# The second MLP of a two-block transformer kernel: both layers as float32r products with sign weights, the second layer turned round

## What is computed

```
def _binarize(w):
    alpha = mean(abs(w), axis=1, keepdims=True)
    bw = alpha * sign(w)
    return w + stop_gradient(bw - w)

def _L1_ffn_ref(x, w1, b1, w2, b2):          # w1 (1024, 256), w2 (256, 1024)
    h = einsum('bsd,hd->bsh', x, _binarize(w1)) + b1
    h = gelu(h, approximate=False)
    return einsum('bsh,dh->bsd', h, _binarize(w2)) + b2

h = _layernorm(x) * (1 + cb) + sb
x = x + gb * _L1_ffn_ref(h, ...)
```

## Time and profile before

| | |
|---|---|
| median of 3 runs | 4103.46 us |
| the profiled execution's own time | 4113.75 us |
| its span, first to last instruction | 4112.0 us |
| mean granted PE clock | 0.918 |
| `mlp1` (b, 0), first product to last | about 34 us, 8 times |
| `mlp1` (b, 1), first product to last | about 38 us, 7 times, with `light` between |
| `mlp1` (7, 1), alone | about 30 us |

### The profile page before, as it was taken

The page is one execution under the profiler, slowest core; times in us unless marked ns, Lnnn a source line. Parts: engine busy times, 40 slices in busy tenths (PEclk is TensorE's granted clock), DMA queues, the critical chain, the costliest instruction groups (busy, mean ns, idle before and its releaser), DMA issues. The chain is left out here.

```text
span 4112.0 us, 81800 instructions
## 1 busy us (share of the span) xinstructions
PE 3470.7 (84%) x30905; PEld 2015.9 (49%) x30905; DVE 2448.6 (60%) x6156; ACT 1925.4 (47%) x4523; POOL 1483.3 (36%) x1807
## 2 busy tenths in 40 slices
PE   7368789997799888997899878998799988999787
PEld 3235544554446544465445544465444654456444
DVE  6755758367563767457573665637674565737652
ACT  5124435554264444554364542654445443645433
POOL 4223442244323442234423543334522444235311
PEclk9579899998899989998999988999999988999889
DMA  7210240002300221002300023002300024000220
GB/s 241 75 37 14 56 109 23 14 28 48 109 17 24 55 79 52 16 12 63 109 16 25 16 64 94 18 22 55 105 26 15 12 63 110 15 25 22 60 65 6
DMA packets 233602, 207.38 MB, mean 50 GB/s; under 512 B 13776, under 2 KB 214224, under 8 KB 233176
## 3 DMA queue, kind: packets, MB, share of 16 engines
q1 hardware_dynamic: 229168, 192.61, 16.9%
q0 software_dynamic: 3328, 8.39, 0.8%
q10 hardware_dynamic: 720, 1.15, 0.1%
HBM read 123.83 MB, written 77.69 MB: 49 GB/s over the span
## 5 line engine op out<-in xcount | busy, mean ns | idle before, releaser
L2379 ACT ACTIVATE arena<-pb 128x512 f32<-128x512 f32 (+3 forms) x1536 | 664.6, 492 | 240.3 <-PE pb L1605 232.7
L2459 POOL TENSOR_TENSOR arena<-arena,small 128x512 f32<-128x512 f32 x256 | 287.0, 1124 | 461.0 <-DVE small L1781 459.6
L2208 ACT ACTIVATE arena<-arena,small 128x256 f32<-128x256 f32 x512 | 255.8, 500 | 387.4 <-DVE small L1764 387.0
L1605 PE MATMUL pb<-arena 98*32 98x512 bf16 (+3 forms) x4608 | 397.7, 339 | 28.4 <-ACT arena L2379 21.7
L1563 PE MATMUL pb<-arena 96*32 96x128 bf16 (+5 forms) x5280 | 369.3, 278 | 58.5 <-DVE arena L2063 24.0
L1623 PE MATMUL pb<-arena,v 128*17 128x512 f32 (+3 forms) x3072 | 381.7, 497 | 26.8 <-POOL arena L2623 17.4
L2623 POOL TENSOR_SCALAR_AFFINE_SELECT arena<-arena 128x256 f32<-128x256 f32 x512 | 217.2, 428 | 462.6 <-ACT arena L2379 459.4
L2063 DVE TENSOR_REDUCE arena<-pb 128x1 f32<-128x512 f32 x512 | 333.3, 684 | 83.3 <-PE pb L1563 81.9
L1764 DVE CUSTOM_DVE_ANT_0 arena<-pb,wmask 128x256 f32<-128x256 f32 x512 | 195.8, 419 | 223.8 <-PE pb L1300 212.4
L1563 PEld LDWEIGHTS pb<-arena 96*32 96x32 bf16 (+1 forms) x5280 | 184.1, 101 | 254.4 <-issue 79.1
L1300 PE MATMUL pb<-arena 128*128 128x256 f32 x1024 | 276.6, 394 | 4.8 <-issue 3.6
(11 more groups left out here) (332 smaller groups left out, 7006.9 us busy)
## 6 DMA issues: line engine op xcount, KB each, us to landing
arena<-split_q SPq DMA_DIRECT2D x64, 384.0 KB, 3.8
arena<-split_k SPq DMA_DIRECT2D x24, 768.0 KB, 6.6
split_q<-arena SPq DMA_DIRECT2D x64, 192.0 KB, 2.3
split_q<-arena SPq DMA_DIRECT2D x96, 128.0 KB, 2.0
split_k<-arena SPq DMA_DIRECT2D x64, 192.0 KB, 2.4
split_k<-arena SPq DMA_DIRECT2D x96, 128.0 KB, 2.1
arena<-split_k SPq DMA_DIRECT2D x24, 384.0 KB, 8.1
xn<-h_d SPq DMA_DIRECT2D x8, 1024.0 KB, 8.8
```

The lines of the kernel that those rows point to most:

```text
L1605: mm = t.matmul(bank[bk][r:r + 32, 0:w_], ka[slot(c, g)][0:KA, h, kt_ * P + r:kt_ * P + r + 32], qa[slot(c, g)][0:KA, h, q0:NH], start=Tru ...
L2208: ins = s.activation(pm[n % 3][:, j], sm[n % 2][:, j], ACT.Exp, bias=nmx[:, 2 * sl + j:2 * sl + j + 1], scale=-1.0, accum_out=sml[:, 2 * s ...
L2379: s.activation(pp[pn % 4][:, h % 2, 0:w_], bank[n % 3][:, 0:w_], ACT.Exp).then_inc(a_exp1, 1)
L2459: g.tensor_tensor(pm[n % 3], pm[n % 3], rcl[:, 2 * sl:2 * sl + 2].unsqueeze(2).broadcast_to([P, 2, 2 * P]), ALU.mult).then_inc(p_norm0, 1)
```

## The change

- `two_valued` no longer forms sign times alpha: it copies the bf16 signs over w; POOL's ten additions, the `wtmp` buffers and one wait in each turn go. The turned weights are written as float32r, alpha is kept in a tile of its own.
- The modulated input is written as float32 (`hT2x`), copied by ACT to float32r (`hT2h`), and DVE writes the remainder as float32r (`hT2l`).
- First layer: for each block four products of 128x512 in float32r (two pieces, high part and remainder) in place of two in float32. ACT's Gelu has alpha as its scale and writes `gt` (two buffers). The result is copied to float32r `gh` (by ACT for c = 0, by DVE for c = 1), and DVE writes the remainder `gl`; both have three buffers.
- Second layer: two blocks behind the first. The sign weights are stationary and `gh`, `gl` move: four products of 128x512 for each block, summed over the eight blocks in two banks (0 and 1 for c = 0; 5 and 6 for c = 1). ACT copies the two sums with alpha into `moT`, PE turns them back in two groups of four, DVE multiplies by the gate and POOL adds, each 128x512, twice instead of four times 128x256.
- The first layer has two banks for c = 0 as before, and one bank (7) instead of three for c = 1.
- The list of steps is the same.

```diff
@@ two_valued (DVE)
-                        v.wait_ge(b_alpha, 2 * m + 2)
-                        if m >= 2:
-                            v.wait_ge(b_add, m - 1)
-                        else:
-                            v.wait_ge(r_h[0], 16 * 2)
-                        v.scalar_tensor_tensor(out=wtmp[m % 2][:, 0:width], in0=sgn[:, c0:c0 + width], scalar=ac, in1=w, op0=ALU.mult,
-                                               op1=ALU.subtract).then_inc(b_sign, 1)
+                        v.tensor_copy(w, sgn[:, c0:c0 + width]).then_inc(b_add, 1)
@@ POOL
-                for m, (w, width, _) in enumerate(BINARY):
-                    g.wait_ge(b_sign, m + 1)
-                    g.tensor_tensor(w, w, wtmp[m % 2][:, 0:width], ALU.add).then_inc(b_add, 1)
@@ banks
-        MLP1_BANKS = {0: (6, 7), 1: (7, 5, 6)}
+        MLP1_NORM, MLP1_W1, MLP1_SUM, MLP1_TURN = ({0: (6, 7), 1: (7, 5)}, {0: (6, 7), 1: (7,)}, {0: (0, 1), 1: (5, 6)}, {0: (6, 7), 1: (7, 5)})
@@ mlp1 (PE)
+                    for m in range(FT + 2):
+                        if m < FT:
+                            bk = MLP1_W1[c][m % len(MLP1_W1[c])]
+                            for w in left[bk]:
+                                t.wait_ge(*w)
+                            for k in range(KD):
+                                t.matmul(bank[bk], w1s[:, k, m * P:(m + 1) * P], hT2h[:, k], start=k == 0, stop=False)
+                                mm = t.matmul(bank[bk], w1s[:, k, m * P:(m + 1) * P], hT2l[:, k], start=False, stop=k == KD - 1)
+                            mm.then_inc(t_w1, 1)
+                            left[bk] = [(a_g, FT * H + m + 1)]
...
+                        if m >= 2:
+                            k = m - 2
+                            t.wait_ge(gl_set, FT * H + k + 1)
+                            for d in range(KD):
+                                t.matmul(bank[sums[d]], w2s[:, k, d * P:(d + 1) * P], gh[:, k % 3], start=k == 0, stop=False)
+                                mm = t.matmul(bank[sums[d]], w2s[:, k, d * P:(d + 1) * P], gl[:, k % 3], start=False, stop=k == FT - 1)
+                            mm.then_inc(t_w2, 1)
+                        yield
...
+                    for u in range(2):
+                        bk = MLP1_TURN[c][u]
                         for w in left[bk]:
                             t.wait_ge(*w)
...
+                        t.wait_ge(a_mo, KD * H + KD)
+                        for i in range(2):
+                            for d in range(KD):
+                                mm = t.transpose(bank[bk][:, (KD * i + d) * P:(KD * i + d + 1) * P], moT[:, d, (2 * u + i) * P:(2 * u + i + 1) * P], ident[:, :])
+                        mm.then_inc(t_mo, 1)
@@ norm_half (DVE); ACT writes hT2x[:, 0] and hT2h
+                    v.tensor_scalar(hT2x[:, 1], bank[banks[1 % len(banks)]], modc[:, 5 * KD + 1, b:b + 1], modc[:, 4 * KD + 1, b:b + 1],
+                                    ALU.mult, ALU.add).then_inc(v_nx, 1)
+                    for k in range(KD):
+                        v.wait_ge(a_n2, KD * H + k + 1)
+                        v.tensor_tensor(hT2l[:, k], hT2x[:, k], hT2h[:, k].bitcast(F32), ALU.subtract).then_inc(v_n2, 1)
@@ mlp1 (DVE)
+                    for m in range(FT + 2):
+                        k = m - 1
+                        if c == 1 and 0 <= k < FT:
+                            v.wait_ge(a_g, FT * H + k + 1)
+                            if k >= 3:
+                                v.wait_ge(t_w2, FT * H + k - 2)
+                            v.tensor_copy(gh[:, k % 3], gt[:, k % 2]).then_inc(gh_set, 1)
+                        if 0 <= k < FT:
+                            v.wait_ge(gh_set, FT * H + k + 1)
+                            if k >= 3:
+                                v.wait_ge(t_w2, FT * H + k - 2)
+                            v.tensor_tensor(gl[:, k % 3], gt[:, k % 2], gh[:, k % 3].bitcast(F32), ALU.subtract).then_inc(gl_set, 1)
+                        yield
@@ mlp1 (ACT)
+                    for m in range(FT + 2):
+                        if m < FT:
+                            s.wait_ge(t_w1, FT * H + m + 1)
+                            if m >= 2:
+                                s.wait_ge(gl_set, FT * H + m - 1)
+                            gelu_tables[0] = True
+                            s.activation(gt[:, m % 2], bank[MLP1_W1[c][m % len(MLP1_W1[c])]], ACT.Gelu, scale=alpha[:, m:m + 1],
+                                         bias=cols[:, C_FB1 + m:C_FB1 + m + 1]).then_inc(a_g, 1)
+                        if c == 0 and m < FT:
+                            s.wait_ge(a_g, FT * H + m + 1)
...
+                            s.activation(gh[:, m % 3], gt[:, m % 2], ACT.Copy).then_inc(gh_set, 1)
+                        yield
```

More of the change, by code:

```diff
@@ L10 @@
 BF16 = mybir.dt.bfloat16
+F32R = mybir.dt.float32r
 I32 = mybir.dt.int32
@@ L1462, in norm_half @@
                         mm.then_inc(t_n2, 1)
[L1463 removed]
+                        left[bk] = [(v_nx if k else a_nx, H + 1)]
                         yield
@@ L1691, in mlp1 @@
                     H = 2 * b + c
[L1692 to L1697, removed]
+                    yield from norm_half(b, c, MLP1_NORM[c])
+                    t.wait_ge(v_n2, KD * H + KD)
+                    sums = MLP1_SUM[c]
+                    for m in range(FT + 2):
[8 more added lines that the diff above has]
+                            left[bk] = [(a_g, FT * H + m + 1)]
+                        if m == 2:
+                            for bk in sums:
+                                for w in left[bk]:
+                                    t.wait_ge(*w)
+                                left[bk] = None
+                        if m >= 2:
[6 more added lines that the diff above has]
+                        yield
@@ L1698, in mlp1 @@
+                    for d in range(KD):
+                        left[sums[d]] = [(a_mo, KD * H + d + 1)]
+                    yield
+                    for u in range(2):
+                        bk = MLP1_TURN[c][u]
                         for w in left[bk]:
                             t.wait_ge(*w)
-                        for k in range(KD):
-                            mm = t.matmul(bank[bk], w1T[:, k, m * P:(m + 1) * P], hT2[:, k], start=k == 0, stop=k == KD - 1)
-                        mm.then_inc(t_w1, 1)
@@ L1720, in mlp1 @@
+                        for i in range(2):
+                            for d in range(KD):
+                                mm = t.transpose(bank[bk][:, (KD * i + d) * P:(KD * i + d + 1) * P], moT[:, d, (2 * u + i) * P:(2 * u + i + 1) * P], ident[:, :])
+                        mm.then_inc(t_mo, 1)
+                        left[bk] = [(v_w2, 2 * H + u + 1)]
+                        yield
+                    for _ in range(3):
                         yield
@@ L2299, in norm_half @@
                         yield
-                    s.wait_ge(t_n2, 2 * H + 1)
-                    s.activation(hT2[:, 0], bank[banks[0]], ACT.Identity, scale=modc[:, 5 * KD, b:b + 1], bias=modc[:, 4 * KD, b:b + 1]).then_inc(a_n2, 1)
+                    s.wait_ge(t_n2, KD * H + 1)
+                    if c == 0:
+                        s.wait_ge(split_out[1][1], 16 * SPLIT_DMAS * (b + 1))
+                    s.activation(hT2x[:, 0], bank[banks[0]], ACT.Identity, scale=modc[:, 5 * KD, b:b + 1], bias=modc[:, 4 * KD, b:b + 1]).then_inc(a_nx, 1)
                     yield
+                    for k in range(KD):
+                        s.wait_ge(v_nx if k else a_nx, H + 1)
+                        s.activation(hT2h[:, k], hT2x[:, k], ACT.Copy).then_inc(a_n2, 1)
                     yield
@@ L2640, in mlp1 @@
                     add_bias(b, c, rows[:, R_B2:R_B2 + D], gates[:, 3])
[L2641 removed]
+                    for _ in range(FT + 2):
                         yield
[L2643 removed]
+                    for _ in range(3):
                         yield
[L2645 to L2647 removed]
+                    for u in range(2):
+                        x = xt[:, TH * c + 2 * u:TH * c + 2 * u + 2]
+                        g.wait_ge(v_w2, 2 * H + u + 1)
+                        g.tensor_tensor(x, x, xadd2[u], ALU.add).then_inc(p_w2, 1)
                         yield
+                    yield
                 take({"start": start, "light": light, "hrows": hrows, "heavy": heavy, "chain": chain, "att": att, "mlp1": mlp1,
```

114 lines of the change are left out of this document (52 added, 62 removed).

## The result

The changed kernel takes 4154.89 us (median of 4 runs, 4149.61 to 4161.64) where the kernel before takes 4105.26 (4 runs on the same chip, 4096.63 to 4116.93): ratio 1.0109, 95% interval 1.009 to 1.0128. It is slower by 1.1%, outside the predicted range of 4048 to 4126. The profiled execution took 4161.64 us, with a span of 4159.9 (before: 4112.0).

What follows compares the result with a forecast made beforehand. PE was taken to bind beside attention, with ACT next to binding beside light. Setup -3.5, attention -48, light +41 and last half -1 made -11.5 from 4103.5, 4092, lowered to 4089 us for hand-over; range 4048 to 4126.

Steps and rivals of the forecast that it cites:

- Which stretches bind, and the sign of each: Halves beside attention: PE binds, its saving counts, -48 us; beside light ACT is next to binding, new waits cost, +41.
- One pass for float32r: PE's first- and second-layer products: a 512-column float32r product takes one pass, 0.216 us, against 0.86 for float32.
- Setup, -3.5: Setup: POOL's 1024-wide additions, which hold up DVE, both go, saving 3.5 us.
- Beside attention, 5.9 to 7.4 earlier at POOL's last addition, 52 in eight halves: Eight halves c = 0: eleventh fill and POOL's last addition come 5.9 to 7.4 us earlier in the layout.
- I take off 0.5 for a lower clock after it: After each half c = 0, PE is less busy and the clock lower: 0.5 us off the gain, leaving 6 us x 8.
- The lead at POOL's last addition taken as the lead of all that follows: After each half c = 0: the lead at POOL's last addition, less 0.5 for clock, counts fully in the total, -48 us.
- Beside light, layout +31: Seven halves c = 1: one-bank and hand-over waits make the ninth scores 0.7 to 5.9 us later each, +31 in all.
- Its clock ... may fall in part of them; I add 1.5 a half: Halves beside light: PE idles three times for 3 to 4 us; clock and DVE meeting POOL add 1.5 each, +10.
- Last half, -1: Half (7, 1), running alone with one bank: second layer nearly hidden, -1 us in all.
- Hand-over, -3: PSUM hand-over, perhaps counted 0.1 us too high at eight places in 15 halves (-6 or so): forecast lowered from 4092 to 4089.
- rival 3: Beside light the clock falls (granted under 0.9), 36 us in seven halves instead of 10: total 4115 to 4129; chance 0.12.
- 14 for clock and contention together: Allowances: 0.5 us per half after attention for clock; 1.5 per half beside light for clock and DVE meeting POOL, +10.

Runs made afterwards that it cites:

- zgap: Changed kernel plus ten unread zero-weight products on PE before each c = 1 first-layer block that would wait behind an exponential round: 4126.16 us, 1.0036 of before.
- zgap_late: Changed kernel plus the zero-weight products of zgap and two unread products beside each first fill of attention halves c = 1 from the eighth: 4105.3 us, 0.9985 of before.
- c0_late: Kernel before with the new form in halves c = 0 alone, plus two unread products beside each first fill of c = 1 from the eighth: 4068.77 us, 0.9899.

## Why the prediction was wrong

- **Which stretches bind, and the sign of each.** Right: beside attention PE's saving counts, beside light it doesn't and the new waits cost.
- **One pass for float32r.** Right: 0.23 us a product, 0.216 assumed.
- **Setup, -3.5.** Right in kind: the operation that was L911, now L909, takes at most 0.285 us in its 19 rounds (2.21 before), and the first turn is 1.9 us earlier.
- **Beside attention, 5.9 to 7.4 earlier at POOL's last addition, 52 in eight halves.** Right: 53.1, and the half takes 30.1 to 31.5 us (29 to 31 stated).
- **"I take off 0.5 for a lower clock after it".** This step failed: the clock took 16.1 us in seven halves, 2.3 each, in the stretch from the row copy to the sixth maximum. I had looked at the stretch after the half for what DVE does, and taken its 0.92 as a state that stays. Before, PE was busy with the second layer up to 613 us; now the half is over at 603.8, and the granted clock is 0.54 and 0.53 in 604 to 614 and 632 to 650.
- **The lead at POOL's last addition taken as the lead of all that follows.** This part of the same step failed too: 8.7 of the lead are gone by the row copy, and padding doesn't bring them back. With 2.2 behind the sixth maximum and 3.0 in b = 7 that makes stretch B +30.0 instead of +4.
- **Beside light, layout +31.** Under-sized: with the clock held it is +40.1. The waits were right (in `zgap` 1.29 for 1.34, and first to last Gelu 25.3 to 27.8 us in seven halves where 27 was stated; 27.2 to 32.6 in the changed kernel, with its clock down). ACT's Gelu with a scale from memory takes 0.78 and not 0.69, and DVE's subtraction 0.83 in the mean. What makes up the other 9 us I didn't take apart.
- **"Its clock ... may fall in part of them; I add 1.5 a half".** This step failed too: 4.2 a half for the clock alone, 29.5 in seven. I had priced what the clock adds inside three gaps, where it stretches every PE step between two Gelus (1.29 to 2.17) for 10 to 17 us in each half.
- **Last half, -1.** +0.4. **Hand-over, -3.** Not found; the prediction's own working has -6 there and takes 3 of it without a reason.

So the mechanism beside light was the planned wait for one bank together with that of rival 3, at 0.12, and its signs are there: the granted clock is 0.81 and 0.77 beside light. Its price for light (36 us) was nearly the measured one, 29.5; but its total of 4115 to 4129 was too low since it kept the loss after the c = 0 half at 0.5 to 1.5. The rule that stands beside it in the prediction (the Trainium skill, TensorE: Matmul & The Clock Gate, A second HAM failure mode) says that PE, idling briefly between groups as it cycles through PSUM banks, makes the clock swing; the trace of after agrees on the idling and the clock, with 96 us at half clock in stretch C where there were none, though PE there has one bank to wait for and none to cycle through.

The account, forecast to result, 4089 to 4155: 26 us in stretch B (12 the clock's, 16.1 against 4 allowed; 14 the rest), 28.6 in stretch C (69.6 for 41; 19.5 the clock's, 29.5 against 10 allowed; 9.1 the layout's), 3 in D, 3 of hand-over, 1.6 in setup, 1.4 in the last half, less 1.1 in A; 1.8 for a base of 4105.3 instead of 4103.5, and 1.7 by which medians and spans differ. B and C are five sixths of it, and the clock's part of them, 31.5 us, is nearly half of the whole miss. `zgap_late`, which props the clock up in both places, takes 51 us off the changed kernel by the ratios (0.0109 + 0.0015, times 4110), where the forecast had allowed 14 for clock and contention together; in it are also 4.7 us that the kernel before pays for its own half clock. The 9 us of the layout are what the clock doesn't explain of C; some of them may still be the clock's, since 14 us at half clock were left there in `zgap`.

The version that beats both is `c0_late`: the new form beside attention only, and PE kept from idling after it, 0.9899 of before (0.9882 to 0.9915).

## What to carry to other kernels

When work is taken off PE, price the clock of what follows, not only of the place itself: list the groups behind the shortened stretch where another engine waits for PE, and what they cost at half clock. If PE's new idle time stands in front of such a group, test with products that nobody reads. What these win is not yet what the change lost, since the old kernel may be paying for half clock too: compare one stretch of equal work, batch by batch, at either clock and in every kernel. Read a lead where the next engine picks it up, and not at the last instruction of the stretch. And a form that saves PE time pays only where PE binds: here one half of the change is worth 0.4% alone (1.0% with the clock kept up), and the other half, which also gave up two of three banks, costs 1.8%.

## What the runs showed of the hardware

- A float32r product of 512 columns starts 0.23 us behind the last at full clock and 0.43 at half; a float32 one takes 0.86 at full clock, about four times as long.
- A conversion of 128x512 float32 to float32r takes 0.63 us on ACT and 0.42 on DVE.
- ACT's Gelu of 128x512 takes 0.78 us with a scale for each partition read from SBUF, 0.69 without.
- The clock stayed at half for 17.1 us in one piece (23.9 in b = 7) with PE busy 16.22 of 18.00 us (granted 0.53, from 632 to 650); in the 18 us before, PE was busy 14.97 at 0.97.
- What half clock costs depends on who waits for PE there: sixteen products that take 3.64 us instead of 1.92 left no delay by the row copy, while 15 to 16 us at half clock behind it cost 3 us in each batch.
- Products with zero weights kept the granted clock up as those with data do (1.00 over 26 us in `zgap`).
